# Narrow diagonal tiles of the pairwise tanh share places of the ring in a fused attention and experts stage

## The reference, cut to what matters

```python
f = jnp.einsum('bih,ha->bia', x, W1[:h])
g = jnp.einsum('bjh,ha->bja', x, W1[h:])
t = jnp.tanh(f[:, :, None, :] + g[:, None, :, :] + b1)        # every query i, every key j, 16 components
scores = jnp.einsum('bija,a->bij', t, w2[:, 0]) + b2[0]
flag = jnp.tril(jnp.ones((n_seq, n_seq), dtype=x.dtype), -1)[None, :, :]
e = jnp.exp(scores) * flag
w = e / (jnp.sum(e, axis=-1, keepdims=True) + 1e-10)
return jnp.einsum('bij,bjh->bih', w, x)
```

## Time and profile before

| | us |
|---|---|
| median of 3 runs | 7842.23 (7842.1 to 7842.64) |
| the profiled execution, its own time | 7842.1 |
| its span | 7840.2 |
| attention stage in the span | about 3650 to 7746 |
| mean granted TensorE clock, as a share of full speed | 0.935 |

### The profile page before, as it was taken

One profiled execution on the slowest core, in us unless ns is written; L12 is line 12 of the kernel. 1 busy time (PEld: TensorE's weight loads), 2 busy tenths in 40 slices (PEclk: granted clock), 3 DMA queues, 4 the chain that ended last, 5 costly groups with the idle time before them and its releaser, 6 DMA issues. The chain is left out here.

```text
span 7840.2 us, 98377 instructions
## 1 busy us (share of the span) xinstructions
PE 6362.3 (81%) x36650; PEld 2230.5 (28%) x36650; DVE 6321.4 (81%) x12662; ACT 5478.7 (70%) x4104; POOL 2073.7 (26%) x1955
## 2 busy tenths in 40 slices
PE   8999999977887799897777767778777877678787
PEld 3333333323443244343211122222222222222223
DVE  7989989976754677587877778989888888889986
ACT  4323333314554555355999999999989999899996
POOL 6777777730001466364000010000000000000002
PEclk9999999978888799898999999999989999899998
DMA  1000000001010000000000000000000000000000
GB/s 52 1 1 1 1 1 1 1 7 30 24 25 7 9 1 1 3 1 7 1 1 1 1 1 1 1 1 1 12 1 1 1 1 1 11 1 1 1 1 22
DMA packets 19014, 45.66 MB, mean 6 GB/s; under 512 B 5735, under 2 KB 7529, under 8 KB 17514
## 3 DMA queue, kind: packets, MB, share of 16 engines
q1 hardware_dynamic: 18538, 39.33, 1.6%
HBM read 14.14 MB, written 8.39 MB: 3 GB/s over the span
## 5 line engine op out<-in xcount | busy, mean ns | idle before, releaser
L2493 ACT ACTIVATE aa_tanh<-aa_tanh 128x4096 f32<-128x4096 f32 (+8 forms) x1280 | 3687.0, 2964 | 118.1 <-DVE aa_tanh L2670 117.9
L2670 DVE TENSOR_SCALAR aa_tanh<-aa_f_times,aa_g_bias 128x1024 f32<-128x1024 f32 (+18 forms) x5120 | 2981.2, 645 | 593.3 <-PE aa_scores L2538 589.1
L2538 PE MATMUL aa_scores<-aa_tanh,aa_w_spread 128*32 128x512 f32 (+8 forms) x18432 | 2175.8, 586 | 830.9 <-ACT aa_tanh L2493 735.2
L2538 PEld LDWEIGHTS aa_scores<-aa_tanh,aa_w_spread 128*32 128x32 f32 x18432 | 583.8, 113 | 2259.2 <-ACT aa_tanh L2493 1054.5
L286 POOL TENSOR_TENSOR near_tap_weights<-near_hat_y_mask,near_hat_x 128x1024 f32<-128x1024 f32 x400 | 935.6, 2368 | 212.8 <-PE near_weights_spread L562 207.3
L576 PE MATMUL near_out_sum<-near_weighted,near_w_out 128*128 128x512 f32 x1408 | 707.4, 625 | 78.6 <-DVE near_weighted L366 77.5
L562 PE MATMUL near_weights_spread<-near_tap_weights,near_spread_consts 36*64 36x512 f32 x6272 | 762.8, 605 | 7.8 <-issue 4.8
L2552 PE MATMUL aa_out_sum<-aa_weights,aa_normed 128*128 128x512 f32 (+3 forms) x1152 | 648.9, 647 | 120.2 <-DVE aa_weights L2679 120.1
L2460 POOL TENSOR_SCALAR aa_group_normed<-x_rows,norm_scale,aa_shift_plus 128x128 f32<-128x128 f32 x96 | 76.4, 807 | 2451.6 <-PE aa_turned L2579 1778.9
L355 DVE TENSOR_TENSOR near_weights_spread<-near_weights_spread,near_values 128x1024 f32<-128x1024 f32 x432 | 529.3, 1225 | 67.3 <-PE near_weights_spread L562 61.3
L366 DVE TENSOR_TENSOR near_weighted<-near_weighted,near_weights_spread 128x1024 f32<-128x1024 f32 x432 | 527.5, 1221 | 20.8 <-DVE near_weights_spread L355 0.5
(11 more groups left out here) (360 smaller groups left out, 7165.9 us busy)
## 6 DMA issues: line engine op xcount, KB each, us to landing
l_taps<-l_scan_in_out SPq DMA_DIRECT2D x256, 64.0 KB, 2.0
x_rows<-in_x SPq DMA_DIRECT2D x4, 2048.0 KB, 14.5
out_x<-x_rows SPq DMA_DIRECT2D x3, 2048.0 KB, 6.3
out_x<-x_rows SPq DMA_DIRECT2D x8, 256.0 KB, 2.0
qa_weights_in<-in_quantum SPq DMA_DIRECT2D x1, 1280.0 KB, 5.8
near_spread_consts<-in_deform_consts SPq DMA_DIRECT2D x1, 805.5 KB, 7.6
l_weights<-in_mamba SPq DMA_DIRECT2D x1, 557.0 KB
consts_sb<-in_consts SPq DMA_DIRECT2D x1, 516.5 KB
```

What stands on the lines that cost most here:

```text
L2493: a.activation(TH[:, (4 * n + tt) % PLACES, 0:length], TH[:, (4 * n + tt) % PLACES, 0:length], ACT.Tanh).then_inc(th_ready, 1)
L2538: last = t.matmul(sp_[32 * q:32 * q + 32, n % 2, s:e], W2S[:, tt, :], TH[:, (4 * n + tt) % PLACES, o + s:o + e], start=tt == 0, stop=tt == ...
L2670: ins = v.tensor_scalar(TH[:, (4 * n + tt) % PLACES, at[q]:at[q] + w - s], FR[:, m % 2, lo + s:CHUNK], GB[:, key:key + 1], None, ALU.add)
```

## The change

Diagonal tiles with at most 512 queries no longer use one place for each slot. `in_a_place(n)` is 2 for the tiles with 512 and 384 queries (two slots side by side in a place) and 4 for those with 256 and 128; it is 1 for all others. `places` lists the places in order, each with its tile and its slots, `place_of` gives a slot's place. ACT takes one tanh for a place, over the columns of all its slots. `sum_ready` and `th_ready` count places; `th_used` still counts slots, and DVE waits for the last slot of the place that lay five places before. DVE fills all slots of a place, then does masks, the output copy and the jobs of all slots of the place five before. An expert sum goes with the first fill of the place six later. PE's loop still goes by slots.

```diff
+        def in_a_place(n):
+            m, j, diagonal, lo, w = shape(n)
+            return 1 if not diagonal or w > BANK else 2 if w > BANK // 2 else 4
+
+        places = [(n, range(tt, tt + in_a_place(n))) for n in range(len(tiles)) for tt in range(0, 4, in_a_place(n))]
+        place_of = {(n, tt): u for u, (n, some) in enumerate(places) for tt in some}
+
+        def place(n, tt):
+            m, j, diagonal, lo, w = shape(n)
+            starts, length = runs_at(w, diagonal)
+            u = place_of[n, tt]
+            return u % PLACES, [(tt - places[u][1][0]) * length + s for s in starts]
...
-        added = {divmod(4 * n + tt + PLACES + 1, 4): x[1] for (n, tt), x in behind.items() if x[0] == "e"}
+        added = {place_of[slot] + PLACES + 1: x[1] for slot, x in behind.items() if x[0] == "e"}
...
-            for n in range(len(tiles)):
+            for u, (n, some) in enumerate(places):
                 m, j, diagonal, lo, w = shape(n)
-                length = runs_at(w, diagonal)[1]
-                for tt in range(4):
-                    a.wait_ge(sum_ready, 1 + 4 * n + tt + 1)
-                    a.activation(TH[:, (4 * n + tt) % PLACES, 0:length], TH[:, (4 * n + tt) % PLACES, 0:length], ACT.Tanh).then_inc(th_ready, 1)
+                length = len(some) * runs_at(w, diagonal)[1]
+                a.wait_ge(sum_ready, 1 + u + 1)
+                a.activation(TH[:, u % PLACES, 0:length], TH[:, u % PLACES, 0:length], ACT.Tanh).then_inc(th_ready, 1)
+                for tt in some:
                     if n and tt == (2 if w >= BANK else 3):
                         exponents(n - 1)
...
-                t.wait_ge(th_ready, 1 + 4 * n + tt + 1)
+                t.wait_ge(th_ready, 1 + place_of[n, tt] + 1)
...
-                if 4 * n + tt >= PLACES:
-                    v.wait_ge(th_used, 1 + 4 * n + tt - PLACES + 1)
+                p, at = place(n, tt)
+                u = place_of[n, tt]
+                if u >= PLACES and tt == places[u][1][0]:
+                    last, some = places[u - PLACES]
+                    v.wait_ge(th_used, 1 + 4 * last + some[-1] + 1)
...
-                for tt in range(4):
-                    fill(n, tt, added.get((n, tt)))
-                    if n >= 2 and tt == 3:
-                        mask(n - 2)
-                    if m and (i, tt) == (2, 1):
-                        keep_out(m - 1)
-                    if 4 * n + tt < PLACES:
-                        continue
-                    slot = divmod(4 * n + tt - PLACES, 4)
+                for tt in some:
+                    fill(n, tt, added.get(u) if tt == some[0] else None)
+                if n >= 2 and 3 in some:
+                    mask(n - 2)
+                if m and i == 2 and 1 in some:
+                    keep_out(m - 1)
+                if u < PLACES:
+                    continue
+                for slot in ((places[u - PLACES][0], tt) for tt in places[u - PLACES][1]):
                     name, at = own_job(*slot) or (None, 0)
```

More of the change, by code:

```diff
@@ L2529, in scores @@
                 m, j, diagonal, lo, w = shape(n)
-                at = runs_at(w, diagonal)[0]
+                p, at = place(n, tt)
                 if tt == 0 and n >= 2:
                     t.wait_ge(e_ready, 1 + n - 1)
-                t.wait_ge(th_ready, 1 + 4 * n + tt + 1)
+                t.wait_ge(th_ready, 1 + place_of[n, tt] + 1)
                 for h in range(0, w, BANK):
@@ L2537, in scores @@
                         o = at[q] - 32 * q * diagonal
-                        last = t.matmul(sp_[32 * q:32 * q + 32, n % 2, s:e], W2S[:, tt, :], TH[:, (4 * n + tt) % PLACES, o + s:o + e], start=tt == 0, stop=tt == 3, tile_position=(0, 32 * q))
+                        last = t.matmul(sp_[32 * q:32 * q + 32, n % 2, s:e], W2S[:, tt, :], TH[:, p, o + s:o + e], start=tt == 0, stop=tt == 3, tile_position=(0, 32 * q))
                 last.then_inc(th_used, 1)
@@ L2669, in fill @@
                     key = 16 * j + 4 * q + tt
-                    ins = v.tensor_scalar(TH[:, (4 * n + tt) % PLACES, at[q]:at[q] + w - s], FR[:, m % 2, lo + s:CHUNK], GB[:, key:key + 1], None, ALU.add)
-                    if q == 3:
+                    ins = v.tensor_scalar(TH[:, p, at[q]:at[q] + w - s], FR[:, m % 2, lo + s:CHUNK], GB[:, key:key + 1], None, ALU.add)
+                    if q == 3 and tt == places[u][1][-1]:
                         ins.then_inc(sum_ready, 1)
@@ L2798, in _ @@
             keep_keys(0)
-            for n in range(len(tiles)):
+            for u, (n, some) in enumerate(places):
                 m, j = tiles[n]
                 i = n - first_of[m]
-                if j == 0:
+                if j == 0 and some[0] == 0:
                     for name in ("f0", "f1", "g"):
                         v.wait_ge(*free(name, m))
-                for tt in range(4):
-                    fill(n, tt, added.get((n, tt)))
-                    if n >= 2 and tt == 3:
-                        mask(n - 2)
-                    if m and (i, tt) == (2, 1):
-                        keep_out(m - 1)
-                    if 4 * n + tt < PLACES:
-                        continue
-                    slot = divmod(4 * n + tt - PLACES, 4)
+                for tt in some:
[7 more added lines that the diff above has]
+                for slot in ((places[u - PLACES][0], tt) for tt in places[u - PLACES][1]):
                     name, at = own_job(*slot) or (None, 0)
@@ L2836, in _ @@
                         gating(G, step)
[L2837 to L2845, removed]
+                if m >= NCH and m % NCH == 0 and i == 5 and 1 in some:
+                    v.wait_ge(st_ready, 1 + 2 * m)
+                    N.moments(v, norm_ch, vv, (m // NCH - 1) * NT, m // NCH * NT)
+                if m > NCH and m % NCH == 1 and i == 2 and 2 in some:
+                    b = m // NCH - 1
+                    if b:
+                        v.wait_ge(mu_ready, 1 + NGI * b)
+                    N.factors(v, norm_ch, ss, b + 1, b * NT, (b + 1) * NT)
+                    v.tensor_scalar(SH1[:, :], N.shift[:, b * NT:(b + 1) * NT], 1.0, None, ALU.add).then_inc(sh_ready, 1)
             mask(len(tiles) - 2)
```

## The result

| | before | changed |
|---|---|---|
| median, us | 7842.76 (6 runs, 7842.1 to 7847.91) | 7791.66 (6 runs, 7789.55 to 7793.38) |
| profiled execution | 7842.1 | 7791.17 |
| its span | 7840.2 | 7789.4 |

The ratio is 0.9933, with a 95% interval of 0.9921 to 0.9946: 51 us faster, where 66 were forecast, inside the range of 7748 to 7818.

The account below looks back on a forecast made before the run. ACT was taken to bound the attention stage, with 134 us of waits for sums and scores. First chunks 44.9, instructions 10.8 and later chunks 10.1 sum to 65.8 us; 7842.1 less that gives 7776 us, range 7748 to 7818.

Parts of the forecast that it names:

- First chunks: Each image's first chunk: the ring reaches further, so ACT starts tile n8 earlier; 44.9 us, ends 20 and 50.
- the walk: Second image's first chunk, tiles n0 to n7 followed through the new order: ACT waits 10.6 us against 20.8.
- Instructions: Diagonal tiles on ACT: 160 of 1280 tanh go at 0.09 us each, 14.4 us, 3.6 of it in first chunks.
- Chunks 1: Second chunk of each image: old ring waits of 2.75 us go, new wait about 1.5; gain 1.25, four times: 5.0.
- Chunks 2: Third chunk of each image: turn copies behind the mask make a new wait of about 4.8 us; loss of 3.1 in all.
- Chunks 3: Last chunk of each image: waits for sums go, one exponent waits 0.3 us longer; gain 2.1 each, 8.2.
- The slower rival: Later chunks: PE held behind DVE's masks costs 10.5 us in each of 12 chunks, 7909 us; chance 0.07.
- The rival in which all waits go: Attention stage: 115 us of waits and 14.4 go, 7713 us, 7749 as its practical form; chance 0.10.
- The signs: Profile after: tanh x1120, busy about 3673 us; ACT's waits for sums and scores about 50 each; DVE's score wait under 589.
- signs of being wrong: First chunks above 82 us or later chunks longer; a chunk 2 score wait over 8 us speaks for the held PE.

Follow-up runs that it names:

- e3: Changed kernel, but in first chunks of images 2 to 4 DVE copies the last output after all of n2 and the mask of n0; 7782.42 us, ratio 0.9923.
- e5: Changed kernel, but slots share places only in the first chunk of each image; 7809.72 us, ratio 0.9952.
- e1: Changed kernel, places still shared, but one tanh for each slot and PE waits for a slot; 7789.81 us, ratio 0.9933.
- e2: Changed kernel, but in shared places DVE does the jobs first and the mask after them; 7765.8 us, ratio 0.9903.
- e9: Changed kernel with only the exponent before a one-place tile moved behind the next tanh after that tile; 7764.04 us, ratio 0.9885.
- e8: Changed kernel with jobs before mask, later output copy, and the exponent before a one-place tile behind the next tanh; 7727.9 us, ratio 0.9846.
- e10: Changed kernel with jobs before mask, later output copy, turns a tile earlier and later exponent together; 7708.79 us, ratio 0.9814.
- e7: Changed kernel with jobs before mask, later output copy, and next chunk's turns one tile earlier in chunks 1 and 2; 7732.81 us, ratio 0.9855.

## Why the prediction was right, and where it was off

- *First chunks, 44.9 us: measured 41.7.* The main steps of the walk hold: DVE's stand at the output copy (8.5 forecast, 7.72 seen), ACT's 4.3 us for the exponent of n2 (4.71), 2.8 between the places of n5 (2.48). Others don't: the exponent of n0 waits 0.89 us and not 2, the 1.7 before (n4,3) are not there, and two waits that the walk had not, 1.34 for the exponent of n3 and 2.73 for that of n4, are. Their sum is 12.2 us of waits where the walk had 10.6. e3 shows the stand as a cause, e5 that these chunks alone bring most of the gain.
- *Instructions, 14.4 us: right as work, worth nothing as time.* The 0.09 us is confirmed by e1, but I put the saving straight on the path. It was given back, in part where ACT waits for PE after a narrow tile and in part where PE waits for a whole place (e1); I had charged 0.3 us of this in each chunk 3, and nothing for it elsewhere but the new wait in chunks 1. This is the term that failed: e1 without it loses nothing (4001.9 and 4001.6 us). The stage fell short by 11.7 us (65.8 forecast, 54.1 measured), so the other terms, 51.4 together, came out about right as a sum, but by errors that cancel: by place, chunks 1 are 12.7 us short and chunks 3 are 4.9 over. That the total is so near is partly luck.
- *Chunks 1, gain 5.0 and 3.6 for instructions: measured a loss of 4.1.* Image 1 gained 2.0, the three images with experts lost about 2 each. The wait that I had at 1.5 us, for the exponent of the 256-query tile, is 1.83 in image 1 and 1.3 to 2.5 in the others. What I had not is a second one in the images with experts, 2.0 to 3.5 us a tile earlier, and 1.1 us for gates. I had only looked at f0 and f1. An expert product takes the PSUM bank that turn1 used, and waits for the copy behind the mask. PE in order of time in the second image's chunk 1, and ACT's wait that follows:

```profile
4888.44 2.08 PE L2609 MATMUL aa_turned<-last_expert_w_centred,aa_group_T 128*128 128x512 f32 x2 [2.62 <-DVE aa_normed_T L2665]
...
4895.80 1.12 ACT L2500 ACTIVATE aa_weights<-aa_scores,aa_weights_in 128x1024 f32<-128x1024 f32 x1 [1.96 <-PE aa_scores L2554]
```

  e2 takes 1.8 to 2.2 us off each of these chunks: the 1.1 us for gates and 0.6 to 1.0 of the waits for scores. The rest stays, since PE passes the expert product and then stands for the copy of f0, which lies behind the fill that the mask still delays. PE at the same place in e2:

```profile
4882.58 2.04 PE L2535 MATMUL aa_turned<-aa_normed_T,aa_weights_in 128*128 128x512 f32 x2 [2.29 <-DVE aa_f_times L2670]
```

- *Chunks 2: a gain of 0.5 forecast, a loss of 0.4 measured,* by two errors that cancel. The long wait was seen correctly and sized too small: 5.69 to 8.16 us instead of 4.8, and with the shorter one before it these chunks have 33.6 us of waits for scores where I had 20.4. e2 shows the mechanism. Against it, ACT's wait for the gates in these chunks (3.7 us in each of three images) went, though I had counted it as one that the change leaves. e5 shows that sharing in the later chunks takes it away; why the gates then come in time is open.
- *Chunks 3, 8.2 and 3.6 us: measured 16.7,* of which 5.6 is again the wait for the gates (1.9 in each of three images). The rest, 11.1, is the forecast.
- *The slower rival* (PE held behind DVE's masks) describes a real mechanism, at 5.7 to 8.2 us in each chunk 2 and 2.0 to 3.5 in chunks 1 of the images with experts instead of 10.5 everywhere, so it did not turn the sign. The rival in which all waits go was far from true, since waits for scores took 73 us back.
- *The signs.* The count of tanhs (1120), their busy time (3671.2 for 3673) and DVE's shorter wait for scores (467.2) came as said. The two waits of ACT did not split as said: about 50 and 50 us forecast, 23.9 for sums and 89.2 for scores measured, and so 13 us more in all. Two signs of being wrong also came: chunks 1 of images 2 to 4 are longer than before, and one wait in a chunk 2 is over 8 us (8.16). So the forecast was right for the first chunks, which bring most of the gain, and for chunks 3 apart from the gates, and not for chunks 1.

## What to carry to other kernels

A ring that holds fixed places is only as deep as its smallest entries make it: here packing small entries into one place let it reach further without more memory, while fusing the instruction on them gained nothing measurable by itself. When a loop is regrouped, look at what each grouped step now waits for ahead of work that others need: here two reorderings of unchanged work (jobs before a wait, a copy later) took another 33 us off the stage, and four took 81. Count an instruction saved on the bound engine only after asking what that engine waits for next.

## What the runs showed that was not expected

The mean duration of one tanh is no measure of its cost on this engine. For the same 1120 instructions it is 3367 ns in the changed kernel, 3386 in e9, 3401 in e8 and 3444 in e10, while the line's busy time rose by only 11 us in e8 and 25 in e10. It does not follow the waits: e7, with 36.8 us of waits for scores instead of 89.2, has 3366 ns. It rose only in the kernels with the later exponent. And two full tanhs (4096 columns) in a row start 3508 to 3509 ns apart in all of these kernels (median, worked out from ACT's order of time), so the longer durations are more overlap with the next instruction and not more time. Why they overlap more is open.
